# The order of scores, transposes and V projection at the head of each half chunk in a vision transformer's attention

## The reference

```
h = tokens(x) + position
h = h + attn0(layernorm(h))     # 16 heads of 64, causal
h = h + ffn(layernorm(h))       # 1024 wide, piecewise linear GELU, fixed point
h = h + attn1(layernorm(h))     # 16 heads of 64, with an output bias
h = h + moe(layernorm(h))       # 8 experts, gates kept above the k-th logit
# attention: softmax(q @ k.T / 8) @ v, then the output projection
```

## Time and profile before

| what | value |
|---|---|
| median of three runs | 1000.7 us (998.15 to 1000.93) |
| the profiled execution | 1000.7 us, its span 998.9 us |
| PE busy | 941.7 us, 94% |
| DVE (VectorE) busy | 579.5 us, 58% |
| ACT (ScalarE) busy | 544.4 us, 54% |
| POOL (GpSimd) busy | 154.6 us, 15% |

### The profile page before, as it was taken

The page is one execution under the profiler, slowest core; times in us unless marked ns, Lnnn a source line. Parts: engine busy times, 40 slices in busy tenths (PEclk is TensorE's granted clock), DMA queues, the critical chain, the costliest instruction groups (busy, mean ns, idle before and its releaser), DMA issues.

```text
span 998.9 us, 18661 instructions
## 1 busy us (share of the span) xinstructions
PE 941.7 (94%) x7159; PEld 870.7 (87%) x7159; DVE 579.5 (58%) x1251; ACT 544.4 (54%) x1570; POOL 154.6 (15%) x173
## 2 busy tenths in 40 slices
PE   5899999999799999999996899999999999999998
PEld 5877888888677878888886898999999999999998
DVE  5466574747899574666664486655354544544342
ACT  4466465643764664646554453756464756555452
POOL 0142122211000121222210000151011111101111
PEclk9999999999999999999999799999999999999999
DMA  7320000002000210000011011101111111100001
GB/s 277 136 76 1 1 2 2 2 1 84 3 1 1 85 43 2 1 2 1 1 43 43 1 62 67 43 1 43 43 44 43 43 43 44 43 1 1 1 14 37
DMA packets 8653, 34.48 MB, mean 35 GB/s; under 512 B 626, under 2 KB 5106, under 8 KB 5236
## 3 DMA queue, kind: packets, MB, share of 16 engines
q1 hardware_dynamic: 8564, 33.28, 9.2%
HBM read 32.06 MB, written 1.22 MB: 33 GB/s over the span
## 4 chain that ended last, share of the span: by engine, by line
issue 31%; PE 24%; POOL 5%; DVE 5%; ACT 2%; POOLq 0%; DVEq 0%; ACTq 0%
PE D L553 8%; PE O L553 7%; POOL h L348 4%; PE O L694 2%; PE T L680 2%; PE S L669 1%; DVE wslot L1094 1%; PE S L553 1%; DVE hid L1481 1%; PE S L663 1%; POOL h L360 1%; ACT hid L1066 1%; ACT work L1062 1%; PE O L799 1%; POOL vbuf L358 1%
## 5 line engine op out<-in xcount | busy, mean ns | idle before, releaser
L1481 DVE TENSOR_TENSOR hid<-work,hid 128x300 fp32r<-128x300 f32 (+1 forms) x256 | 139.3, 564 | 200.1 <-ACT hid L1066 200.0
L553 PE MATMUL O<-hid,wslot 128*128 128x300 f32 (+3 forms) x1680 | 242.4, 302 | 0.0
L553 PEld LDWEIGHTS O<-hid,wslot 128*128 128x128 f32 x1680 | 234.7, 190 | 0.6
L553 PE MATMUL D<-xn,wslot 128*128 128x300 f32 (+3 forms) x1368 | 224.4, 309 | 4.6 <-ACT work L950 2.6
L553 PEld LDWEIGHTS D<-xn,wslot 128*128 128x128 f32 x1368 | 198.8, 190 | 10.0 <-ACT work L950 2.9
L1062 ACT ACTIVATE work<-D,prm 128x300 f32<-128x300 f32 (+1 forms) x128 | 66.7, 521 | 185.6 <-PE D L553 185.5
L960 ACT ACTIVATE probs<-S,negmax 111x111 f32<-111x111 f32 (+1 forms) x352 | 117.5, 359 | 53.4 <-DVE negmax L1242 53.2
L532 POOL TENSOR_TENSOR probs<-probs,rsum 111x444 f32<-111x444 f32 (+1 forms) x88 | 80.9, 920 | 379.8 <-DVE rsum L1250 379.8
L553 PE MATMUL S<-xn,wslot 128*128 128x300 f32 (+3 forms) x864 | 137.1, 306 | 0.0
L553 PEld LDWEIGHTS S<-xn,wslot 128*128 128x128 f32 x864 | 126.4, 193 | 0.3
L1242 DVE TENSOR_REDUCE negmax<-S 111x4 f32<-111x444 f32 (+1 forms) x88 | 52.6, 600 | 72.1 <-PE S L669 72.1
(11 more groups left out here) (163 smaller groups left out, 1158.7 us busy)
## 6 DMA issues: line engine op xcount, KB each, us to landing
raw<-in_moe SPq DMA_DIRECT2D x16, 1024.0 KB, 4.8
raw<-in_attn SPq DMA_DIRECT2D x8, 1024.0 KB, 4.9
work<-in_x SPq DMA_DIRECT2D x2, 1008.0 KB, 7.9
raw<-in_ffn SPq DMA_DIRECT2D x1, 1024.0 KB, 4.7
w2f<-in_ffn SPq DMA_DIRECT2D x1, 1024.0 KB, 6.8
raw<-in_x SPq DMA_DIRECT2D x2, 504.0 KB, 5.5
out<-h SPq DMA_DIRECT2D x3, 300.0 KB, 2.7
raw<-in_w_lin SPq DMA_DIRECT2D x1, 768.0 KB, 4.1
```

What stands on the lines that cost most here:

```text
L553: mm = pe.matmul(psum, a, b, start=(first and k == 0), stop=(k == 3 * n - 1))
L1481: nc.vector.tensor_tensor(moe_hid(s, 1), moe_g(s)[:, 0:w], moe_hid(s, 0).bitcast(F32), ALU.subtract).then_inc(m_hid, 1)
```

## The change

At a first unit of a half TensorE does transposes(2u-2) before scores(u) and no longer after; in unit 0, where there is nothing to transpose, it does project_v(0) before scores(0). On VectorE move_t(2u-2) goes ahead of row_max(2u) at the same units; in unit 0 its order stays. All other units, engines and DMAs keep their order.

```diff
+        def half_begins(u):
+            return u < NUNIT and place_in_half(u)[0] == 0
@@ TensorE, attention
-                    if u < NUNIT:
+                    if half_begins(u):
+                        if u == 0:
+                            project_v(u)
+                        else:
+                            transposes(2 * u - 2)
                         scores(u)
-                    if 0 <= u - 1 < NUNIT:
-                        transposes(2 * u - 2)
-                    if u < NUNIT:
+                    else:
+                        if u < NUNIT:
+                            scores(u)
+                        if 0 <= u - 1 < NUNIT:
+                            transposes(2 * u - 2)
+                    if 0 < u < NUNIT:
                         project_v(u)
@@ VectorE, attention
-                    if u < NUNIT:
+                    if half_begins(u):
+                        if u > 0:
+                            move_t(2 * u - 2)
                         row_max(2 * u)
-                    if 0 <= u - 1 < NUNIT:
-                        move_t(2 * u - 2)
+                    else:
+                        if u < NUNIT:
+                            row_max(2 * u)
+                        if 0 <= u - 1 < NUNIT:
+                            move_t(2 * u - 2)
```

## The result

| | before | after |
|---|---|---|
| median | 1000.02 us (998.15 to 1002.25, 6 runs) | 1007.63 us (1005.1 to 1010.37, 6 runs) |
| ratio, 95% interval | | 1.0077 [1.0052, 1.0101] |
| profiled execution, its span | 1000.7, 998.9 us | 1006.73, 1004.9 us |
| TensorE's mean granted clock | 0.990 | 0.984 |
| PE busy | 941.7 us | 946.5 us |

The kernel became 0.8% slower. That is over the top of my range (1005.3) and over three times the loss that I forecast. The first thing to see is the row of the other engines: they did the same work in the same time. TensorE ran the same 7159 matmuls in 4.8 us more of busy time. A new order moves work and adds waits, but it adds no matmuls, so something else made them take longer.

The account below looks back on a forecast made before the run. TensorE was taken as the busiest engine, with 8.3 us of waits for Q/K copies and VectorE's chain to the values limiting the gain. First attention +0.91, second +1.00, unit 0 +0.5: +2.4 us, 1003.1 us, range 1000.2 to 1005.3.

Parts of the forecast that it names:

- Bound and stall: TensorE busiest; its mask matmul waits 16 times for ScalarE's last Q/K copy, 8.3 us, at most 0.8% to gain.
- Part 1: Transposes ahead of scores on TensorE, 7 places an attention: 0.41 plus 0.09 fits the 0.54 stall, later TensorE work 0.41 earlier.
- Part 2: VectorE's copy ahead of the row maximum: values later at units 3, 9, 12, 18, 0.41 gained at 6 and 15.
- The limit of 2.88: Values start no earlier than 2.88 us after the start of the unit's first row maximum, whatever TensorE saves.
- Units 20 and 21: Unit 20's gain does not arrive, since unit 21's exponentials wait behind a weight copy: 0, lower bound -0.4 in each attention.
- Part 3: Unit 0, V before scores: second attention +0.5 us, as unit 1's scores wait for exponentials; first attention 0.
- ends in a wait that is there anyway: First attention, unit 1: unit 0's delay falls into 0.99 us of idle for GpSimd's weight split, priced at 0.
- What TensorE saved before the values turns into waiting for VectorE: Units 3, 9, 12, 18: the copy delays the maximum 0.53, so values come 0.44, 0.32, 0.44, 0.53 later in the first attention.
- unit 18 stood on the limit, +0.53: Unit 18's values already waited 2.88 us after the maximum, so the copy's whole 0.53 us delays them.
- (b): Rival: scores wait until the last transpose has landed, 0.14 later at 14 places, 2.0 us more: 1005.1 us; chance 0.17.
- (c): Rival: some 0.15 of give at eight late places and in unit 0 absorbs 1.4 us: 1001.7 us; chance 0.15.
- (a): Rival: the stall is simply filled, 3.2 us gained in each attention, 6.4 in all: 994.3 us; chance 0.08.

Follow-up runs that it names:

- e9_whole: The changed kernel unedited, run again on one chip with e10_whole_not18; 1.0060 of the kernel before.
- e2_unit0: The changed kernel with only unit 0 changed (V before the scores in both attentions), all other units in old order; 1.0004 of the kernel before (1000.7 us).
- e1: The changed kernel with unit 0 back in its old order, so only the first units of a half are changed; 1.0053 of the kernel before (1005.7 us).
- e6: e3, but in unit 18 of both attentions VectorE copies before the row maximum; 1.0004 of the kernel before.
- e10_whole_not18: The changed kernel, but VectorE keeps its old order (row maximum, then copy) in unit 18; 1.0017 of the kernel before.
- e5: e1, but VectorE keeps its old order (row maximum, then copy) in unit 18; 1.0008 of the kernel before.
- e7: e1 plus dummy matmuls on TensorE ahead of the first Q/K block: 3 at unit 3, 2 at 9 and 12, 5 at 18; 1.0012 of the kernel before (1001.6 us).
- e3: e1, but VectorE keeps its old order in every unit, so only TensorE's transposes move; 0.9975 of the kernel before.

## Why the prediction was wrong

- **Bound and stall: right.** PE's wait for the Q/K copy fell from 8.3 to 1.1 us (I wrote under 2).
- **Part 1, TensorE: right in its mechanism.** Values 4.59 after the scores in unit 6 (I wrote 4.56), -0.38 in unit 15 (-0.41). Transposes, change of mode and scores fit into the stall. Alone this part gains 0.25%.
- **Part 2, VectorE: right to 0.03 us a unit.** +0.42, +0.32, +0.43, +0.52 in units 3, 9, 12, 18 (forecast +0.44, +0.32, +0.44, +0.53), and +0.52 in unit 3 of the second attention, where the quarters stand in front. The limit of 2.88 held wherever the values waited for the copy (2.87 to 2.89). Units 20 and 21 gave -0.12 and -0.09 in place of 0.
- **Part 3, unit 0: right, a little smaller.** +0.32 in place of +0.5, with the wait for exponentials that was named; unit 0's scores came 0.70 later, not 0.84 to 0.93. In the first attention the longer idle time of unit 1 was priced at 0, "ends in a wait that is there anyway"; on the schedule that holds (e9_whole, without low clock there, adds nothing in unit 1), but the profile of after has low clock behind it, 1.55 us. e2_unit0 bounds what it costs in the median: under 1.4 us, the schedule included.
- **The step that failed** is "What TensorE saved before the values turns into waiting for VectorE" and the sum's "unit 18 stood on the limit, +0.53". I priced a wait at its own length. Three idle times of TensorE in unit 18, 0.42 before the scores, 0.43 before the second transposes and 0.33 before the values, became 0.31 and one hole of 1.38, and in each of the four traces that have this hole (after, e1, e6, e9) the granted clock halved behind it in one of the two attentions. That term was missing from the sum and from every rival. Its size is 3.3 us by e10_whole_not18 against e9_whole, 3.4 by e5 against e1, 4.1 with all holes filled (e7 against e1), and 1.8 where e6 adds it to e3. It is a new cost, not a mis-sized one, which is why the range, made of the bounds of the terms that I had, could not hold it. With the 2.1 of schedule it makes 5 to 6 of the 7.6 us; the rest is the low clock in unit 1 and the spread between executions and chips (the same kernel lost 6.0 us as e9_whole).
- **Rivals.** (b) is refuted: the drain adds nothing. (c) is refuted: nothing was absorbed. (a) was wrong for this change but points at what TensorE's part gives by itself, 2 to 3 us and not the 6.4 of my estimate (whose terms, 6 x 0.41 + 0.4 + 0.5, are 3.4 for an attention and not 3.2), since units 3, 9, 12 and 18 are held by VectorE even then.

**Open.** Which executions get the stretch, and what a hole must be like. Behind the hole of 1.38 us each of the four traces shows low clock in one attention and not in the other, for 6.8 to 10.2 us, beginning 0.4 to 1.6 us after the values. The hole of 1.1 us in unit 3 of the second attention was followed by it in one trace of five, and the pieces of 0.94 and 0.63 us in unit 1 of the first attention in three of four (after, e2 and e10, not e9). Length alone does not decide: ahead of the first attention TensorE idles 2.6 to 2.7 us in every kernel, and in the traces of before, after and e6 the clock stayed full behind it. Nor do the runs separate the length of the one hole from the 0.5 us by which the unit's idle time grew.

## What to carry to other kernels

When a ready operation is to pass a waiting one, decide it for each engine by itself: on TensorE the transposes filled a hole, on VectorE their copy pushed back the row maximum on which the next unit hangs; the first alone wins, both together lose. Then add up where TensorE's idle time will lie and not only how much it is, for short waits that are joined into a longer one can cost several times their length in clock. It was so here: 0.5 us more of idle time in unit 18, most of it in one hole, and 3 to 5 us lost behind that in a trace. And before a stall is filled, look for the chain that ends next: here the layer norm in front of the maximum, and moving it in one unit of each attention gave as much again (0.24%) as TensorE's whole part of the reorder (0.25%).

## What was unexpected of the hardware

- A single idle piece of 1.38 us on a TensorE otherwise 94% busy was followed by 6.8 to 10.2 us at 1.2 GHz at four of its eight places in four traces, 4.7 us lost for each 10.2. Pieces of up to 1.1 us mostly were not followed by it (none in e5_halves_not18, one in e9_whole). The Trainium skill, "TensorE: Matmul & The Clock Gate" (A second HAM failure mode: psum-queue depth-cycling), says of another kernel that TensorE's frequent short idle times between groups of matmuls make its clock swing between its two states. The traces here agree in kind: the fall came behind idle time between groups, here one piece of 1.38 us (once 1.10) with a shorter one of 0.30 to 0.68 ahead of it.
- Matmuls whose results nobody uses made the kernel faster: e7_halves_fill ran 0.4% faster than e1_halves with 48 more of them recorded and the values of the filled units starting as long after their scores as before, to 0.02 us.
- A 128-column fp32 dummy matmul is recorded as two passes: in e7_halves_fill five of them are x10, 1.29 us modelled and 1.05 from their start to that of the next group, 0.21 each.
